# An audio tower block on one core: 258-column tiles with split weights against 512-token tiles with plain fp32 matmuls, logarithmic mixer and 32-row scores

## The reference

```
h = tok(x)                                   # x: 8 x 256 x 128
h = h + attn(layernorm(h))
h = h + ffn(layernorm(h))

def tok(x):                                  # a gated recurrence over time, kept in logarithms
    zf, zi, zh = x @ Wf + bf, x @ Wi + bi, x @ Wh + bh
    diff = softplus(-zf) - softplus(-zi)
    log_f, log_i = -softplus(diff), -softplus(-diff)
    log_val = concat([log(0.5), log_i + log_g(zh)]);  a = concat([0, log_f])
    return exp(a + cumlogsumexp(log_val - a))          # 8 x 257 x 128

def attn(x):                                 # 8 heads of 16; batch b attends to batch b +- 4
    scores = q k' / sqrt(128);  return softmax(scores) v

def ffn(x):                                  # a shared expert and 16 routed ones, top 2, all computed
    t = swiglu5(x @ w1 + b1)                 # clip gate and up, gate * sigmoid(alpha * gate) * scale * (up + shift)
    y = sum over experts of cw[n, e] * (t_e @ w2_e + b2_e);  return y + shared
```

## Time and profile before

| | us |
|---|---|
| median of 3 runs (390.0 to 390.88) | 390.45 |
| the profiled execution: its span, from the first instruction to the last | 388.2 |
| PE busy (2160 matmul records) | 316.8 |
| VectorE busy | 298.8 |
| ScalarE busy | 243.1 |
| GpSimd busy | 158.3 |
| mean granted PE clock, share of full speed | 0.918 |

### The profile page before, as it was taken

One profiled execution on the slowest core, in us unless ns is written; L12 is line 12 of the kernel. 1 busy time (PEld: TensorE's weight loads), 2 busy tenths in 40 slices (PEclk: granted clock), 3 DMA queues, 4 the chain that ended last, 5 costly groups with the idle time before them and its releaser, 6 DMA issues. The chain is left out here.

```text
span 388.2 us, 6049 instructions
## 1 busy us (share of the span) xinstructions
PE 316.8 (82%) x2160; PEld 258.7 (67%) x2160; DVE 298.8 (77%) x500; ACT 243.1 (63%) x412; POOL 158.3 (41%) x125
## 2 busy tenths in 40 slices
PE   3427028986968999999899999979999998879873
PEld 1105027854667878788588787968787887768752
DVE  7894646722579969978998999887976788887990
ACT  2684521542684858597598685675773877485751
POOL 1000372101032874744348577342234445357752
PEclk9767755798986999999999999989999999999998
DMA  7500850000390000008400000075000000000000
GB/s 270 221 0 0 220 80 2 0 3 0 117 183 0 2 3 1 0 3 218 56 28 2 2 3 0 2 207 67 28 2 0 3 2 0 0 31 3 0 1 27
DMA packets 12414, 17.30 MB, mean 45 GB/s; under 512 B 984, under 2 KB 9184, under 8 KB 12256
## 3 DMA queue, kind: packets, MB, share of 16 engines
q1 hardware_dynamic: 12384, 16.91, 17.6%
HBM read 11.63 MB, written 5.28 MB: 44 GB/s over the span
## 5 line engine op out<-in xcount | busy, mean ns | idle before, releaser
L506 POOL TENSOR_TENSOR te<-tbuf,ubuf 128x516 f32<-128x516 f32 x52 | 73.8, 1424 | 50.4 <-DVE tbuf L882 27.6
L956 PE MATMUL slot<-xh,w1h 128*128 128x258 f32 x208 | 64.7, 311 | 13.0 <-DVE xl L865 4.0
L495 POOL TENSOR_TENSOR ubuf<-ubuf,cwb 128x516 f32<-128x516 f32 x24 | 34.3, 1429 | 67.2 <-ACT cwb L659 48.9
L956 PE MATMUL slot<-xh,w1l 128*128 128x258 f32 x208 | 59.9, 288 | 0.0
L956 PE MATMUL slot<-xl,w1h 128*128 128x258 f32 x208 | 59.8, 288 | 0.0
L956 PE MATMUL slot<-te,w 128*128 128x258 f32 x208 | 50.7, 393 | 4.2 <-POOL te L506 3.5
L956 PEld LDWEIGHTS slot<-xh,w1h 128*128 128x128 f32 x208 | 40.3, 194 | 19.4 <-issue 14.0
L882 DVE SCALAR_TENSOR_TENSOR tbuf<-tbuf,gbuf 128x516 f32<-128x516 f32 x52 | 48.3, 935 | 6.0 <-ACT tbuf L666 5.6
L781 DVE TENSOR_REDUCE mx<-slot 128x2 f32<-128x514 f32 x64 | 41.6, 687 | 12.6 <-PE slot L956 12.4
L956 PEld LDWEIGHTS slot<-te,w 128*128 128x128 f32 x208 | 39.6, 195 | 12.8 <-POOL te L506 6.4
L646 ACT ACTIVATE gbuf<-slot,cst 128x516 f32<-128x516 f32 x52 | 35.8, 690 | 19.2 <-PE slot L956 16.8
(11 more groups left out here) (161 smaller groups left out, 614.6 us busy)
## 6 DMA issues: line engine op xcount, KB each, us to landing
qs<-spill SPq DMA_DIRECT2D x12, 258.0 KB, 4.5
ks<-spill SPq DMA_DIRECT2D x24, 129.0 KB, 5.9
spill<-qhl SPq DMA_DIRECT2D x4, 516.0 KB, 2.8
spill<-khl SPq DMA_DIRECT2D x4, 516.0 KB, 3.4
pt<-in_w SPq DMA_DIRECT2D x1, 1664.0 KB, 9.5
xt<-in_x SPq DMA_DIRECT2D x4, 256.0 KB, 5.4
out<-osb SPq DMA_DIRECT2D x8, 128.0 KB
te<-in_sel SPq DMA_DIRECT2D x1, 832.0 KB, 11.0
```

What stands on the lines that cost most here:

```text
L495: g.tensor_tensor(ubuf[:, c % NB, :, :], ubuf[:, c % NB, :, :], cwb[:, :, :], ALU.mult).then_inc(S["ucw"], 1)
L506: g.tensor_tensor(te[:, c % NTE, :, :], tbuf[:, c % NB, :, :], ubuf[:, c % NB, :, :], ALU.mult)\
L956: return nc.tensor.matmul(out_, lhsT, rhs, start=start, stop=stop, **k)
```

## The change

The change replaces the kernel. The work stays in four units of two batches, on the same engines, again with an order written out in `AT` (new tables) and a table `BANK_OF` that gives each matmul result one of eight single banks. The parts:

- **Tiles.** W = 512: a unit's 2 x 256 positions stand in one tile and one bank. The first position (constant for all) is taken out of the units and is computed once for all eight batches, in pieces whose names begin with z (`zv` to `zstore`), at 8 columns each.
- **Mixer.** zf, zi, zh by the same three matmuls; sums of logarithms are made by PE (`lsum` 5, `wsum` 3, `wm` 1, `fsum` 3 matmuls of 512 columns), with softplus as Abs, Exp, Ln on ScalarE; two scans on VectorE read PSUM or SBUF; the reciprocals are gone.
- **Attention.** q and k stay fp32 and in SBUF: the spill and the stacking are gone. Masked copies `km`, `qm` let one matmul of 32 rows make the scores of two heads, 512 columns (`mx`, `st`); the pieces are pairs of such matmuls on neighbouring groups of 32 rows. The maxima come in as a second 32-row matmul (`nm`). `pv` is as before, with 256 columns. The denominator is inverted by Ln and Exp on ScalarE.
- **Feed-forward.** Partitions stand for (expert, eighth), so that 12 routed chunks share one set of parameters and one weighting tile `cwb` for a unit; the shared expert is the 13th. Gate and up are one fp32 matmul of 512 columns each. Bias and shift come in through a row of ones in `xn2`. Chunks are taken in pairs (k = 0 to 6): elementwise instructions are 1024 wide. Who takes what: `GATE_BY`, `UP_BY`, `CW_BY`, `TE_BY`. "V" is clipped out of PSUM by VectorE, "AV" is copied by ScalarE and clipped in SBUF by VectorE, "AG" copied by ScalarE and clipped by GpSimd. `down` accumulates all chunks in one bank on top of the residual.
- **Set-up.** Two copies of w1 (1.7 MB each) are loaded and subtracted by GpSimd (`w1p`, `w1s`).

```diff
-W = N + 1
+W = 2 * T
+GATE_BY = ("V", "AV", "V", "AV", "V", "AV", "V")
+UP_BY = ("AG", "AG", "V", "AG", "V", "V", "V")
+CW_BY = ("G", "G", "G", "G", "G", "G", "")
+TE_BY = ("G", "V", "G", "V", "G", "V", "V")
+NY, NV, NT = 3, 3, 4
+NPT = 4
...
-        slot_mem = [ctx.enter_context(nc.psum_tensor(f"slot{i}", [P, 2, 512], F32)) for i in range(NSLOT)]
+        memory = [ctx.enter_context(nc.psum_tensor(f"bank{i}", [P, 512], F32)) for i in range(BANKS)]
...
+            def w1p(u, k):
+                ...
+                g.tensor_tensor(w1[:, cols], w1[:, cols], w1_rows[:, cols], ALU.subtract).then_inc(s_w1, 1)
...
+            def weigh(u, k):
+                ...
+                g.tensor_tensor(vr[:, n % NV, :, :], vr[:, n % NV, :, :],
+                                cwb[:, u % 2, :].unsqueeze(1).to_broadcast([P, 2, W]), ALU.mult).then_inc(S["vcg"], 1)
...
+            def pt_(u, s, c, t):
+                ...
+                last = a(pt[:, n % NPT, 2 * t:2 * t + 2, :].rearrange("p i t -> p (i t)"), ps.bank("st", u, s, c, t)[:, :],
+                         ACT.Exp, scale=SCORE_SCALE)
...
+            def mr(u, s, c, t):
+                ...
+                last = v.tensor_reduce(mxt[:, s, c, 32 * t:32 * t + 2],
+                                       ps.bank("mx", u, s, c, t)[:, :].rearrange("p (i t) -> p i t", i=2), AX_X, ALU.max)
...
+            def gate_evict(u, c):
+                ...
+                last = v.tensor_scalar(yr[:, n % NY, c % 2, :], ps.bank("g", u, c)[:, :], fpar[:, GHI, r:r + 1],
+                                       fpar[:, GLO, r:r + 1], ALU.min, ALU.max)
...
+            def gate_clip(u, k):
+                ...
+                v.tensor_scalar(y, y, fpar[:, GHI, r:r + 1], fpar[:, GLO, r:r + 1], ALU.min, ALU.max).then_inc(S["gcv"], 1)
...
+            def gg(u, k):
+                ...
+                v.scalar_tensor_tensor(t_, t_, 1.0, halves(k, yr, n % NY), ALU.add, ALU.mult).then_inc(S["gg"], 1)
...
-            def max_(st, u, s, c, t):
-                ...
-                for i in range(2):
-                    last = mm(slot(st, name)[:, i, 0:W], qs[0:KR, s, t, c * P:(c + 1) * P], ks[0:KR, 1 - s, t, i, :])
+            def mx(u, s, c, h):
+                ...
+                for t in (2 * h, 2 * h + 1):
+                    rows = slice(32 * t, 32 * t + 32)
+                    ps.fill(mm(ps.bank("mx", u, s, c, t)[:, :], qt[rows, s, c * P:(c + 1) * P],
+                               km[rows, 1 - s, :, :].rearrange("p i t -> p (i t)")), "mx", u, s, c, t)
...
+            def st(u, s, c, h):
+                ...
+                for t in (2 * h, 2 * h + 1):
+                    rows = slice(32 * t, 32 * t + 32)
+                    mm(ps.bank("st", u, s, c, t)[:, :], kt[rows, 1 - s, c * P:(c + 1) * P],
+                       qm[rows, s, :, :].rearrange("p i t -> p (i t)"), stop=False)
+                ge(pe, "nm", 2 * u + s + 1)
+                for t in (2 * h, 2 * h + 1):
+                    rows = slice(32 * t, 32 * t + 32)
+                    ps.fill(mm(ps.bank("st", u, s, c, t)[:, :], const("onesr")[rows, :],
+                               nm[rows, s, :, :].rearrange("p i t -> p (i t)"), start=False, stop=True), "st", u, s, c, t)
...
-                    mm(o, w1h[:, k, c, :], xh[:, s, :], stop=False)
-                    mm(o, w1h[:, k, c, :], xl[:, s, :], start=False, stop=False)
-                    last = mm(o, w1l[:, k, c, :], xh[:, s, :], start=False)
+            def half_(u, c, name, kind):
+                ...
+                ps.fill(mm(ps.bank(name, u, c)[:, :], w1_of(c, kind), xn2[:, u % 2, :]), name, u, c)
...
+            def down(u, k):
+                n = NP * u + k
+                te_done(pe, n)
+                pe.wait_ge(s_w2s, 2)
+                for c in chunks(k):
+                    last = mm(ps.bank("y0", u)[:, :], w2[:, c, :], tr[:, n % NT, c % 2, :], start=False, stop=(c == NC - 1),
+                              skip_group_check=True)
```

More of the change, by code:

```diff
@@ L122 @@
-PIECES = [p for u in range(UNITS) for p in unit_pieces(u)]
+    name, u, *numbers = piece
+    k = numbers[0] if numbers else 0
+    if name in ("ge", "ue"):
+        by = (GATE_BY if name == "ge" else UP_BY)[k // 2]
+        return engine == by[0]
+    if name in ("gc", "uc"):
+        by = (GATE_BY if name == "gc" else UP_BY)[k]
+        return len(by) > 1 and engine == by[1]
+    if name == "vc":
+        return engine == CW_BY[k]
+    if name == "te":
+        return engine == TE_BY[k]
+    return engine in BY[name]
@@ L224, in build, with filled_by @@
-def build(nc, x_in, consts_in, sel_in, w1_in, w2_in, spill, out):
+BANK_OF = (
[9 rows of a table added]
+)
+def order(engine):
+    if not AT:
+        return PARTS[engine]
+    return [p for _, p in sorted(zip(AT[engine], PARTS[engine], strict=True), key=lambda x: x[0])]
+def filled_by(piece):
+    name, u, *numbers = piece
+    if name in ("mx", "st"):
+        return [(name, u, *numbers[:2], 2 * numbers[2] + i) for i in range(2)]
+    one_bank = ("z", "lsum", "fsum", "center", "var", "q", "k", "v", "nmt", "o0", "gate", "cwb", "y0", "g", "u", "out",
+                "zv", "zc", "zvar", "zgate", "zcw", "zg", "zd", "zout")
+    return [piece] if name in one_bank else []
@@ L306, in const @@
+        memory = [ctx.enter_context(nc.psum_tensor(f"bank{i}", [P, 512], F32)) for i in range(BANKS)]
+        full = [sem(f"psum_full{i}") for i in range(BANKS)]
+        free = [sem(f"psum_free{i}") for i in range(BANKS)]
+        ps = Psum(memory, full, free)
         def const(name):
@@ L1143, in out_ @@
[L1143 to L1151 removed]
+                ps.take(pe, "z", u, j)
@@ new lines, in gate, with cwb_ @@
+            def gate(u):
+                ge(pe, "one", u + 1)
+                pe.wait_ge(s_w1, W1_SET)
+                ps.take(pe, "gate", u)
+                for k in range(4):
+                    last = mm(ps.bank("gate", u)[:, k * E:(k + 1) * E], xn2[:, u % 2, k * P:(k + 1) * P], gate_w)
+                ps.fill(last, "gate", u)
+            def cwb_(u):
+                ge(pe, "cwr", 4 * u + 4)
+                ps.take(pe, "cwb", u)
+                for k in range(4):
+                    last = mm(ps.bank("cwb", u)[:, k * P:(k + 1) * P], cwr[:, k, :, :].rearrange("p e r -> p (e r)"), ident)
+                ps.fill(last, "cwb", u)
@@ new lines, in zd @@
+            def zd(u):
+                ps.released(pe, "zcw", 0)
+                ps.take(pe, "zd", 0)
+                o = ps.bank("zd", 0)[:, 0:B]
+                mm(o, ident, zt[:, 0, :], stop=False)
+                mm(o, const("b2"), zt[:, 5, :], start=False, stop=False)
+                ge(pe, "zte", 1)
+                pe.wait_ge(s_w2s, 2)
+                for c in range(NC):
+                    last = mm(o, w2[:, c, :], zy[:, 2, c, :], start=False, stop=(c == NC - 1))
+                ps.fill(last, "zd", 0)
```

1688 lines of the change are left out of this document (873 added, 815 removed), and 116 rows, old and new, of tables (AT, BANK_OF, BY, ENGINES).

## The result

The changed kernel takes 397.31 us in the median (four runs, 396.57 to 397.86); the kernel before took 390.66 beside it (390.0 to 391.82). The ratio is 1.017, with a 95% interval of 1.0146 to 1.0194: **slower by 1.7%**, where 375 us were forecast. The profiled run spans 395.2 us against 388.2 before.

The account below looks back on a forecast made before the run. PE and VectorE held the old body; PE was to bound the changed kernel. First scores 45, remaining PE work 309.0, waits 14 and end 5 gave a 373 us span; with the median 2.2 above, 375 us, range 348 to 415.

Parts of the forecast that it names:

- the start: Before the first scores: PE's 40 matmuls and the chain each about 43 us, plus 2 for mutual waiting, 45 us.
- the waits of PE: After the first scores: 14 us, as 5 in first-unit maxima, 5 in last-unit feed-forward, 4 elsewhere; low end 4, high 68.
- What bounds the kernel: Body before held by PE and VectorE together, start by a chain; after the change, other engines far below PE's 343.0 us.
- The price of a matmul: On PE: an fp32 matmul of 512 columns takes 0.85 us, two records of 0.425; 248 of them take 210.8 us.
- The 32-row matmuls: Attention scores on PE: 192 matmuls, pairs side by side and partly overlapping the next, 75 slots, 63.8 us.
- four together throughout: Rival in attention scores: four 32-row matmuls always together, 48 slots, 23 us less, 352 us; chance 0.14.
- the end's 5: End of the kernel: last matmul, pass over the last result, transposes, copy and stores, 5 us.
- a clock that drops in the middle: Sign listed under what would show the forecast wrong: PE's clock falling mid-kernel; no size given.
- The rival on the other side: VectorE held behind GpSimd: 54 us more VectorE, half reaching PE, 402 us; chance 0.28 shared with pairs not overlapping.
- The engines' sums: Busy time forecast for the other engines over the whole kernel: VectorE 194 us, ScalarE 202, GpSimd 147.
- The chances: For the whole kernel against the one before: faster 0.62, same 0.04, slower 0.34.
- on the line: Measured time indistinguishable from no change, 389.7 to 391.2 us; chance 0.03.

Follow-up runs that it names:

- e4_same_rows: The changed kernel with all 32-row score matmuls on array rows 0 to 31, so none run side by side; 602.5 us, ratio 1.515 to the kernel before.
- e1_hilo: The changed kernel with gate and up as three float32r passes over high and low parts; 409.31 us, ratio 1.041 to the kernel before.

## Why the prediction was wrong

The forecast was 375 us and faster; it is 397 and slower, inside the range. Two steps failed: the start, where PE's work and the chain were taken to hide each other, and the waits of PE, which had nothing for half clock and for short waits inside busy time. Step by step:

- **What bounds the kernel** was right: PE has 93% of the span, VectorE 58%.
- **The price of a matmul** was 1% low: 512 fp32 columns take 0.859 us (two records 0.429 apart) in place of 0.85. Over 248 of them that is 2.2 us.
- **The 32-row matmuls** were sized well. All their stretches together take 70.5 us with the tiling changes in them, where I had 63.8 and, for both kinds of tiling, 9.0 of changes. Pairs run side by side, and four together where a pair on the other rows follows directly: a pair alone hands over to the next piece after 1.06 us, four after 1.07, where four one by one would take 3.44, 3.2 times as long. Two pairs for the exponentials with their two second pairs, eight products, take 1.94 us, so that a further four add 0.87. So the mechanism of the rival "four together throughout" is there, but the list has it in too few places. The Trainium skill ("TensorE: Matmul & The Clock Gate", Part 3, measured speedup) has 3.07 times for four; the trace is near it with 3.2, but many stretches here are not of four.
- **The first scores**, forecast at 45: 51.24. This step failed. I took PE's 40 matmuls and the chain through the other engines as both 43 us and gave them 2 us for waiting on each other; PE stood idle for 12.4 of the first 45 us, 6.9 of them after its first matmul at 5.48. The 40 matmuls and the 2.5 us at half clock came out as forecast or nearly so (40 and 3.1). Two rows of equal length that hand over to each other are not hidden behind each other.
- **Waits of PE, 14 us.** As idle time this was nearly right: the windows from 45 to 360 leave 7 us idle and those after it 10, of which I had the end's 5 apart. But the step failed in what it left out. It had nothing for the clock. 17.0 us of the body ran at half clock and cost about 8.5, although I named "a clock that drops in the middle" as a sign and had the kernel before with a mean clock of 0.918. Some 9 us more lie inside busy time, as short waits between records that the modelled ends cover: six halves in a row take 5.48 us to the next piece in the median of four such rows, where six at cadence are 5.15.
- **The rival on the other side** gave 402 and is close in time, not in cause. Its mechanism is there (1651 ns in place of 1220), and "half of that reaches PE" was the wrong part: PE's waits that VectorE ended come to some 6 us, and taking the cause away gave 1.6%.
- **The engines' sums**: ScalarE 202 forecast, 184 measured; GpSimd 147 and 141.5; VectorE 194 and 228.5, of which 31 us went with the weighting, the waiting behind GpSimd that the forecast left to the rival, and 6 are the 56 clips out of PSUM at 0.80 us in place of 0.69.
- **The chances** by their own parts are 0.03 on the line and 0.35 slower, where the forecast's last sum has 0.04 and 0.34.

The missing 22 us are thus: the start 6, the columns 2, half clock 8 or 9, and 6 in the stream of PE (the 9 of short waits, less some 3 by which idle time and the 32-row matmuls stayed under the forecast). None of them is large, and nearly all have one sign, since the forecast was a sum of PE's floors with a small allowance. And the reason that the change as such didn't pay is in its first line: at 200 to 240 before, PE was the fullest engine; the change took 129 us from VectorE and ScalarE and 17 from GpSimd, and gave PE 62 of work at full clock, more than the 55 that came off its idle time and half clock.

## What to carry to other kernels

When PE is the bound, forecast three sums and not one: its work at full clock, what half clock takes, and its idle time; the kernel before has all three in its trace. Ask of each stretch by itself whether one engine bounds it: work taken from PE came off one for one in the attention, and only 8 us of 56 did in the feed-forward, where 30 came back as half clock and 18 as waiting. Before spending array time on exactness, ask what the number is for: a maximum that only shifts an exponent needs none, and rounding it turned a kernel that was 1.7% slower than the one before into one 4.6% faster.

## What the runs showed of the hardware

- PE at 96% busy had a mean clock of 0.812 while its 32-row matmuls ran one after the other (`e4_same_rows`), and in the changed kernel, where the same matmuls run two and four side by side, it was 0.977. The span was 198.7 us longer, and about half of that was lost to the clock.
- In a row of 52 records of 8 columns (7.2 us, changed kernel) the clock fell to 1.2 GHz after 4.3 us and stayed there for 6.8 us. In a row of 104 (19.5 us, `e1_hilo`) it fell after 2.7 us. There was no idle time before either.
- Between executions of one kernel, 1 us more lost to half clock went with 0.9 us more of span (fit within kernels, 86 executions).
- Two fp32 matmuls of 32 rows on different rows hand over to the next piece after 1.06 us, four after 1.07, and four more add 0.87; full-height ones follow each other by 0.86. Two pairs on the same rows take 1.92. (The changes of tiling before and behind them are in the 1.06, 1.07 and 1.92.)
- Three float32r passes of 512 columns take 0.70 us in a row and 0.87 standing alone between other pieces (median of nine), so that beside an fp32 matmul at 0.86 (0.96 alone) little is left of their advantage.
- VectorE's two-input instruction of 1024 columns, 1.22 us in the median, took 1.74 to 3.37 in nine of 24 cases in the changed kernel, and each of these ended 1.07 to 1.09 us after the GpSimd instruction that it lay beside; its mean fell from 1.65 to 1.22 when the weighting was left out.
